# The turn of the row maxima and the copy of its result, set further up in an attention unit

## The reference

```python
att = jnp.einsum('bthd,bThd->bhtT', q, k) / math.sqrt(HD)
causal = jnp.triu(jnp.ones((Tx, Tx), bool), 1)
att = jnp.where(causal, -jnp.inf, att)
att = jax.nn.softmax(att, axis=-1)
out = jnp.einsum('bhtT,bThd->bthd', att, v).reshape(Bx, Tx, Cx)
return out @ Wo + bo
```

## Time and profile before

| | |
|---|---|
| median of 3 runs | 2137.15 us (2135.57 to 2139.05) |
| profiled execution, its time | 2139.61 us |
| its span | 2137.9 us |
| mean granted TensorE clock | 0.894 |
| TensorE busy | 1770.4 us, 83% |
| VectorE busy | 1354.6 us, 63% |
| ScalarE busy | 1167.6 us, 55% |
| GpSimd busy | 893.4 us, 42% |

### The profile page before, as it was taken

One profiled execution on the slowest core, in us unless ns is written; L12 is line 12 of the kernel. 1 busy time (PEld: TensorE's weight loads), 2 busy tenths in 40 slices (PEclk: granted clock), 3 DMA queues, 4 the chain that ended last, 5 costly groups with the idle time before them and its releaser, 6 DMA issues. The chain is left out here.

```text
span 2137.9 us, 41383 instructions
## 1 busy us (share of the span) xinstructions
PE 1770.4 (83%) x12676; PEld 915.7 (43%) x12676; DVE 1354.6 (63%) x2378; ACT 1167.6 (55%) x2826; POOL 893.4 (42%) x1047
## 2 busy tenths in 40 slices
PE   7559999967168673999999965699999999999996
PEld 4324444425157461232333313355555555555552
DVE  5646777722212443788888813578788888878872
ACT  2226676641023241677777740477767777767771
POOL 5424544531410651011111111567666676666660
PEclk9759999986579785899999985799999999999996
DMA  4312222210033121122222221011111111111110
GB/s 128 111 47 80 74 78 86 73 55 2 29 108 90 47 81 62 52 85 76 81 86 80 78 91 62 23 34 37 38 32 36 45 40 37 33 38 33 47 36 13
DMA packets 93685, 126.53 MB, mean 59 GB/s; under 512 B 17041, under 2 KB 56852, under 8 KB 93457
## 3 DMA queue, kind: packets, MB, share of 16 engines
q1 hardware_dynamic: 91536, 121.11, 17.9%
q0 software_dynamic: 2048, 4.16, 0.7%
HBM read 66.28 MB, written 43.52 MB: 51 GB/s over the span
## 5 line engine op out<-in xcount | busy, mean ns | idle before, releaser
L1025 DVE TENSOR_REDUCE M_sb<-banks 128x1 f32<-128x512 f32 (+3 forms) x1024 | 539.8, 584 | 201.0 <-PE banks L825 114.9
L911 ACT ACTIVATE probs_sb<-banks 128x512 f32<-128x512 f32 (+3 forms) x1024 | 469.1, 521 | 195.7 <-PE banks L851 192.0
L822 PE MATMUL banks<-K_sb,Q_sb 72*128 72x512 bf16 (+3 forms) x1024 | 360.4, 358 | 67.7 <-PEq L344 57.9
L851 PE MATMUL banks<-Q_sb,K_sb 75*128 75x512 bf16 (+3 forms) x1024 | 345.8, 345 | 8.1 <-DMA Q_sb<-mrows_sb 4.1
L866 PE MATMUL banks<-probs_sb,V_sb 128*32 128x512 f32 (+3 forms) x2048 | 234.5, 529 | 11.8 <-issue 7.7
L822 PEld LDWEIGHTS banks<-K_sb,Q_sb 72*128 72x128 bf16 x1024 | 100.7, 99 | 319.5 <-DVE M_sb L1025 172.5
L1820 ACT ACTIVATE l_p_sb<-banks,l_nb_sb,l_inv_sb 128x128 f32<-128x128 f32 x512 | 228.0, 465 | 12.9 <-DVE l_nb_sb L1992 12.7
L1906 POOL TENSOR_TENSOR l_pn_sb<-l_p_sb,l_rs_sb 128x512 f32<-128x512 f32 x128 | 150.1, 1172 | 149.6 <-DVE l_rs_sb L1998 148.1
L1898 POOL TENSOR_TENSOR l_inv_sb<-l_clip_sb,l_minus_half_sb 128x16 f32<-128x16 f32 x64 | 186.2, 2910 | 57.1 <-DVE l_clip_sb L1967 55.2
L1891 POOL TENSOR_TENSOR l_ts_sb<-l_t_sb 128x1024 f32<-128x1024 f32 x64 | 153.3, 2395 | 32.6 <-DVE l_kn_sb L1976 16.9
L851 PEld LDWEIGHTS banks<-Q_sb,K_sb 75*128 75x128 bf16 x1024 | 100.0, 99 | 96.1 <-ACT probs_sb L911 21.3
(11 more groups left out here) (202 smaller groups left out, 3356.7 us busy)
## 6 DMA issues: line engine op xcount, KB each, us to landing
Q_sb<-qk_dram SPq DMA_DIRECT2D x192, 96.0 KB
o_dram<-osum_sb SPq DMA_DIRECT2D x64, 256.0 KB, 4.9
l_vs_sb<-l_vt_sb SPq DMA_DIRECT2D x112, 128.0 KB, 2.3
qk_dram<-parts_sb SPq DMA_DIRECT2D x96, 128.0 KB
K_sb<-qk_dram SPq DMA_DIRECT2D x32, 288.0 KB
opack_sb<-o_dram SPq DMA_DIRECT2D x16, 256.0 KB, 3.4
inverse_sb<-s_dram SPq DMA_DIRECT2D x16, 256.0 KB, 3.3
ew_sb<-in_ew SPq DMA_DIRECT2D x16, 256.0 KB, 3.5
```

The source lines that it names most:

```text
L822: mm = pe.matmul(out[:, 0:width], g.Q[0:RK, slot, h, k * P:(k + 1) * P], g.K[0:RK, slot, hk(h), 0:width], start=True, stop=not causal)
L851: pe.matmul(SB[ring % 3][:, t0:N], g.K[0:RM, q, hk(h), k * P:(k + 1) * P], g.Q[0:RM, q, h, t0:N], start=True, stop=True).then_inc(s["b_sco ...
L911: act.activation(g.probs[:, k, h, t0:N], SB[ring % 3][:, t0:N], ACT.Exp, scale=scale)\
L1025: dve.reduce_max(g.M[:, u % 2, k, h:h + 1], SA[ring % 3][:, 0:width], AX.X, negate=True)\
```

## The change

The turn on TensorE stands behind b_tile(1, 0), three heads further up; pv(q, 0) stays where it is, behind b_tile(1, 3). The copy on ScalarE stands behind the exp of (1, 2), two exps further up, so that one exp lies between copy_out and it. The waits are the same, and nothing is added or taken away.

```diff
                             b_tile(i, q, k, h)
-                            if (k, h) == (1, 3) and m is not None:
+                            if (k, h) == (1, 0) and m is not None:
                                 turn_max(i, m)
                             if h == 3 and k:
                                 pv(i, q, k - 1)
...
                             exp(i, q, k, h)
                             if (k, h) == (1, 1) and not (first and q == 0):
                                 copy_out(i, q - 1)
-                            if (k, h) == (2, 0) and m is not None:
+                            if (k, h) == (1, 2) and m is not None:
                                 copy_rows(i, m)
```

## The result

The changed kernel takes 2153.2 us (2151.3 to 2160.0) against 2136.4 (2135.5 to 2139.1): a ratio of 1.0083, with a 95% interval of 1.0058 to 1.0107. It is slower, by about the amount that was forecast (2151.7). The profiled execution's span is 2149.6 us against 2137.9, so the profile explains 11.7 us of the 16.8 between the medians; the profiled execution is also the fastest of the changed kernel's four. The rest is not located in this profile; that of the first experiment tells where such differences lie.

What follows compares the result with a forecast made beforehand. TensorE was taken to bound the kernel, back to back in the attention stages except where pv(q, 0) waits for the output copy. Terms 8.45 + 8.7 - 2.7 = +14.5 us gave 2151.7 us by the median, range 2141 to 2160.

Steps and rivals of the forecast that it cites:

- Reading of the old place: End of group k = 1: the output copy releases pv(q, 0), and the turn lies for nothing in that wait.
- (a): The turn leaves the end of the group: gains nothing by itself, as what follows still waits for the output copy.
- (c): Turn delays second score, its exp, output copy, pv(q, 0): layer 1 0.30 us a unit, 8.45 us; layer 0 8.7 us.
- (b): The turn set behind the group's first head, where TensorE is back to back: costs about 0.35 us there.
- the price X: The turn's cost behind the group's first head: 0.09 us in, 0.26 through and out, about 0.35; bounds 0.21 and 0.53.
- (d): Row copy two exps earlier on ScalarE: 1.94 us to the end of exp(1,3), its bank needed after 2.6 us.
- the ring of banks: Three banks for the scores: predicted to hold with the earlier row copy, 1.94 us against 2.6 us.
- (e): Rows' DMA issued about 1 us earlier gains nothing; longer units shorten nine layer 1 waits, 9 x 0.30 = 2.7 us back.
- The bound of 5.8: Upper bound on what comes back: all weight-load idle on the rows' DMA in nine units of layer 1, 5.8 us.
- rival 1: pv(q, 0) waits for TensorE's own order, so leaving the group's end repays the new place: 2131.4 us; chance 0.07.
- The dear turn: Turn behind the group's first head costs 0.53 us, 10.6 us more in 59 units: 2162.3 us; chance 0.12.
- the cheap one: Turn behind the group's first head costs only its streaming, 0.21 us: 2144.7 us, or 2140.2; chance 0.18.

Runs made afterwards that it cites:

- the first experiment: The kernel before with only the turn moved behind b_tile(1, 0), the row copy left where it was: 2153.2 us against 2138.2, ratio 1.0076.

## Why the prediction was right, and where it was off

**Reading of the old place: right.** In the kernel before the turn lay for nothing in the wait for the output copy. Twice the turn there left the units as long as they were, and with the copy moved away pv started behind the turn.

**(a) and (c), the chain: right.** pv(q, 0) follows the copy's end by 0.06 to 0.07 us in every unit of the changed kernel, and of the kernels with the turn at (1, 0) alone and with the doubled one. One head later, behind the second score, the loss is gone; with the copy ahead of the second exp, three quarters of it. The room of 0.05 us in layer 1 that (c) gave to ScalarE is what was found: 0.41 of price, 0.36 of delay.

**(b), the price X: the mis-sized term.** It was 0.41 us, not 0.35. The way in, 0.09, was exact. The way out was set at 0.26, as half of 0.52 us at a granted clock of 0.50. It is 0.32: only the streaming halves with the clock. At full clock that is 0.21, and 0.11 us stay; the row at half clock has 0.43 of streaming and 0.09. The value lies between the bounds of 0.21 and 0.53. The 0.06 us repeat in nearly all units: layer 1 got 0.36 us a unit and not 0.30. Layer 0 got 0.29 (q = 2) to 0.37 (q = 0) and not 0.25; and in the units of q = 3 it is 0.56 (10.34 to 10.90 us) and not 0.45: there the turn does wait for VectorE, 0.48 us behind the score instead of 0.25. All in all 20.3 us between the copies where the prediction had 17.15.

The rule that the Trainium skill states in TensorEngine Tiling (Array Packing), Key Properties, that a change of the tiling mode drains TensorE, was weighed there without a term. The rows agree with it as far as the place has a price: in between full-width scores the turn pays 0.09 us on its way in and 0.11 on its way out; beside pv the way out is 0.11 to 0.12 us in all from weights to weights, less than the streaming. By this rule of the Trainium skill that is the change of tiling mode, shared with pv in the old place and paid twice in the new one. That the mode is the cause, and not the number of weight columns as such, no run here shows.

**(d), the ring of banks: right.** The row copy made no difference.

**(e), what the loads give back: right in kind, too small.** The shorter waits come from the longer units and not from the earlier issue. With long units and late rows the waits went; with units of the old length and early rows they stayed; with shorter units they grew. But the amount was 7.6 us and not 2.7. Against the kernels without such waits, layer by layer between the copies, they cost 6.5 us in layer 1 and 3.1 in layer 0 before the change, and 1.3 and 0.6 after it. With the copy moved up it was 13.4 and 8.2 in the kernel before and 5.7 and 12.8 in the changed one: there the loads took most of the expected gain. The prediction counted only the rows' waits, in 9 units, each shrinking by one unit's delay. It left out the five for K, those of layer 0, and that the delays of several units may add up for a load that starts no later; this last is argued, not shown. The bound of 5.8 was the rows' alone and too low. One of the prediction's own signs of being wrong, that the waits vanish where the K load is in front, nearly came: they went in seven of the nine units, though not in the one it had read the earlier trace rows, which still waits 0.61 us. The rows did go out 1.5 us earlier against the first score of the group, but the first experiment shows that the waits go without that.

So the forecast met the time because **two errors cancel**: +17.15 - 2.7 = 14.5 was predicted for the units, +20.3 - 7.6 = 12.7 is what they show. That is luck, and so is the nearness of 14.5 to the 16.8 us between the medians, of which 4 lie outside the units, where the prediction had nothing. The sign and the mechanism did not depend on that.

**The rivals.** The turn's place alone (rival 1) fell: leaving the end gave nothing back, as pv(q, 0) still started 0.07 us behind the copy. The dear turn had 0.53 and the cheap one 0.21; 0.41 lies between, with streaming plus two small overheads.

## What to carry to other kernels

Work that lies in a wait is free, and moving it is a loss unless the wait moves with it: find what ends the wait (here an output copy, from two times in 60 units, where the profile named something else) and move that. Before an instruction goes into a back-to-back row, look at which engine's chain starts behind it; one head to either side decided over the whole loss. When a unit gets longer or shorter, count what the loads behind it take or give: here they returned 7.6 of 20.3 us, and ate most of a gain.

## What the runs showed of the hardware

**Three engines for three copies.** A load whose outermost count is 3 kept the DMA share at 0.18 to 0.21, about 3 of 16 engines, at 74 to 86 GB/s; with 8 or 24 outermost the share was 0.38 to 0.50 at 107 to 164 GB/s. The stores with an outermost count of 4 ran at 0.27 and 92 to 96 GB/s, about 4 of 16. The Trainium skill states this in DMA: Bandwidth & Descriptors, Rules for kernel authors: an outermost dimension of a size below 16, such as a leading broadcast of some copies, confines the DMA to at most that many engines. The trace agrees; the edit that spread both the loads and the store of K was worth 47 us here.

**A wait that costs more than its length.** In the kernel with the turn at (1, 1) one score found its K not yet loaded, and TensorE stood for 1.98 us:

```profile
1000.05 0.39 PE L822 MATMUL banks<-K_sb,Q_sb 72*128 72x512 bf16 x1 [1.98 <-DMA K_sb<-qk_dram]
```

Stretches around it (columns as above):

```profile
999.00:1000.00 1.00, 0.00 (x0) 0.00 (x0) 0.00 (x0) 0.00 (x0) 0.22 (x1) 1.00 0.09 35
1000.00:1001.00 1.00, 0.55 (x2) 0.26 (x3) 0.52 (x1) 0.00 (x0) 0.00 (x0) 0.72 0.21 84
1001.00:1006.00 5.00, 5.00 (x13) 1.66 (x16) 2.23 (x5) 2.04 (x4) 0.00 (x0) 0.50 0.19 76
```

After nearly two idle microseconds the granted clock fell to 0.72 and to 0.50, its 1.2 GHz level, and stayed there for over five, though the engine was busy throughout. The unit took 18.4 us; the other units of its place took 13.1 to 13.5.

**An overhead that did not scale with the clock.** The way from the turn to the next score has 0.09 us over its streaming at 1.2 GHz and 0.11 at 2.4 GHz. A price read at one level should be split into columns and rest before it is taken to the other.
